# The last two tiles of a cross-attention stream in another order, and four weight splits on GpSimd

## The chip, the cores and the metric

The kernel runs on 1 core of one Trainium2 chip. The metric is the device time of one execution in microseconds.

## What is computed

A perceiver block: 256 query rows of 512 values (`x`), a context of 25088 rows of 512 values. Three residual steps, each on the layer-normalized `x`. The change touches the end of the first and the start of the second.

```python
x = x + xattn(layernorm(x), ctx, ctx, Wq, bq, Wk, bk, Wv, bv)   # sigmoid(qp kp^T / sqrt(128)) (ctx Wv^T + bv)
x = x + attn(layernorm(x), ...)    # 16 heads of 32, a shared rope part, causal softmax
x = x + ffn(layernorm(x), ...)     # 8 experts, the best one per row
```

The output must have float32 accuracy. The large matrix products therefore run on operands split into a high part, rounded to fp32r, and a low part (value minus high part), with three products: high by high, high by low, low by high.

## The kernel before

**The stream.** The context comes in 49 tiles (b = 0 to 48, `last` = 48) of 512 rows. Each is loaded twice, transposed (`rawt`) and as rows (`rawn`), each in two halves. For a tile the kernel

- splits the transposed tile into `th` (ScalarE, `copy`, line 401) and `tl` (VectorE, line 651), and the rows into `nh` (line 401) and `nl` (line 662);
- forms the keys on TensorE (`keys`, 12 matmuls of 512 columns) and splits them into `kph` (ScalarE, line 423) and `kpl` (VectorE, line 667);
- forms the scores against the queries (`scores`, 12 matmuls of 256 columns, banks 2 and 3: bank 2 holds context rows j = 0, 1, bank 3 holds j = 2, 3);
- takes the sigmoid into `zf` (ScalarE, line 432, one half for each bank), splits it into `zh` (line 401) and `zl` (VectorE, line 672), and adds `zf` to `zacc` (line 677), from which the sums of weights `zsum` come at the end;
- adds weights by context rows to the sums `y` (`value`): 4 row groups j, 2 halves r of the queries (bank 4 for r = 0, bank 5 for r = 1), 3 products i, so 24 matmuls of 512 columns.

All matmuls are issued by the helper `mm` and so have line 1009 in the profile. The second half of the context rows of tile 48 is split into `th` and `tl`, which are free by then.

**The order.** Each engine has one queue, filled in the order in which the program's block of that engine is written, with semaphore waits (`wait_ge`) between instructions; `Steps` only names the semaphore values. In the stream TensorE does scores(b), keys(b+1), values(b). At the end (lines 1160 on) the order is written out: `row_values(last - 1, 0)`, `scores(last)`, three products of row half 1 of tile 47, `last_values(0)` (12 products), four more of row half 1; then the sums of row half 0 go to `y_s` (ScalarE), are turned (`transposes`, line 1101), split into `yTh` and `yTl`, and multiplied by the value weights (`project_v(0)`), among the rest of row half 1's products. When the last product is done (`av1`), ScalarE copies row half 1 to `y_s` in two pieces, TensorE turns them (line 1229), then turns the normalized `h_s` of row half 0 (line 1101), then does `project_v(1)`.

**Behind the stream.** `norm_stats` and `norm_rows` (VectorE, with the square root `root` on ScalarE) give the normalized rows `h_s` from the projected sums; `latents` projects them; `query(t)` multiplies `hqh`, `hql` by the query weights, split into `wqh` (ScalarE) and `wql` (VectorE, line 682) while the stream ends; `query_copies` move the queries from PSUM into `qa`. The output weights `wo_s` are split into `woh` (ScalarE) and `wol` (VectorE, line 757) behind the stream and read by `project_o`. GpSimd only fills three tiles at the start (lines 394 to 396).

The DMA of `wo_s` waits on SyncE's queue for the last split of tile 48 (`n_split(last, 1)`); behind it stand the loads of the down weights `wds`. An activation of a function of another table than the last one loads the table (line 404, `table`, does it ahead of need).

Of the kernel before, what the change touches and what calls it, by code (L numbers as in the profile page):

```python
# [5 lines left out]
ALU = mybir.AluOpType  # L6
# [8 lines left out]
T = 256  # L15
# [39 lines left out]
def signals(nc, ctx, NB):  # L55
# [36 lines left out]
    s.zh, s.zl, s.za = (steps(n, tiles) for n in ("zh", "zl", "za"))  # L92
# [3 lines left out]
    s.zs, s.zs1, s.zr = (steps(n, ["z"]) for n in ("zs", "zs1", "zr"))  # L96
# [38 lines left out]
def program(nc, x, ctxn, ctxt, wkt, wqt, wvt, bqk, bv, kvd, kup, vup, wq, qrope, krope, wo, gate, wg, wu, wd,  # L135
# [3 lines left out]
    with ExitStack() as ctx:  # L139
# [252 lines left out]
        @block.gpsimd  # L392
        def _(e):
            e.memset(wz[:], 0.0).then_inc(*s.wz.mark("wz"))  # L394
            e.memset(zacc[:], 0.0).then_inc(*s.pz.mark("zacc"))
            e.memset(one_s[:], 1.0).then_inc(*s.pz.mark("one"))

        @block.scalar
        def _(e):
# [25 lines left out]
            def weights(b):  # L425
# [7 lines left out]
                e.wait_ge(*s.zf.of((b, 1)))  # L433
                copy(zh[b % 2][:], zf[:]).then_inc(*s.zh.mark(b))

            def query_weights(k):
# [5 lines left out]
                copy(flat(wqh[:, n]), flat(wq_s[:, n]), -0.125).then_inc(*s.wqh.mark(k))  # L442
# [23 lines left out]
            for b in range(NB - 1):  # L466
# [9 lines left out]
                split_n(b + 1, 0)  # L476
                split_n(b + 1, 1)
# [6 lines left out]
            weights(last)  # L484
# [27 lines left out]
            def query_copies(t, bk):  # L512
                e.wait_ge(*s.q.of(t))
                for i in (0, 2):
                    copy(qa[64 * (i % 2):64 * (i % 2) + 32, 2 * t + i // 2, :],
                         bank(bk)[32 * i:32 * i + 32, 0:T]).then_inc(*s.qaa.mark((t, i)))
# [4 lines left out]
            sum_turned(0, 0, slice(0, 4), 6)  # L521
            e.wait_ge(*s.dwo.of("w"))
            output_weights(0)
            root(0)
# [12 lines left out]
            root(1)  # L537
            e.wait_ge(*s.lnt.of((1, 3)))
# [9 lines left out]
            table(ACT.Exp)  # L548
# [95 lines left out]
        def _(e):  # L644
# [28 lines left out]

            def weight_sum(b):
# [3 lines left out]

            def query_weights(k):
                n = slice(2 * k, 2 * k + 2)  # L680
                e.wait_ge(*s.wqh.of(k))
                e.scalar_tensor_tensor(out=flat(wql[:, n]), in0=flat(wq_s[:, n]), scalar=-0.125, in1=flat(wqh[:, n]),
                                       op0=ALU.mult, op1=ALU.subtract).then_inc(*s.wql.mark(k))
# [35 lines left out]
            for b in range(NB - 1):  # L719
# [5 lines left out]
                if b + 2 < NB:  # L725
                    split_t(b + 2, 0)
                    split_t(b + 2, 1)
                split_n(b + 1, 0)
                split_n(b + 1, 1)
                if b >= NB - 3:  # L730
                    query_weights(b - (NB - 3))
# [4 lines left out]
            weights(last)  # L736
            weight_sum(last)
            e.wait_ge(*s.za.of(last))
            e.tensor_reduce(zsum[:], zacc[:].rearrange("p (j n) -> p n j", j=4), AX_X, ALU.add).then_inc(*s.zs.mark("z"))
# [13 lines left out]

            def output_weights(k):
                n = slice(2 * k, 2 * k + 2)
# [715 lines left out]
```

## Time and profile before

| | us |
|---|---|
| time, median of 3 runs | 574.36 (573.89 to 574.87) |
| profiled execution | 574.13 |
| span of the profiled execution | 572.3 |
| TensorE busy | 566.7 (99%) |
| VectorE busy | 462.9 (81%) |
| ScalarE busy | 403.1 (70%) |
| GpSimd busy | 1.7 |

The profile is that of one execution. Times in it are microseconds from the start of the span. In the page and the answers PE is TensorE's matmuls, PEld its weight loads, DVE is VectorE, ACT ScalarE, POOL GpSimd, SPq SyncE's DMA queue. The stream ends at about 487, the heads of the attention begin at about 505, and the experts run from 530 to the end.

### The profile page before, as it was taken

Reading aid. Unit: us, or ns where it says so; the run is one execution under the profiler, and the core shown is the slowest. Engines: PE = TensorE matmul, PEld = TensorE weight load, DVE = VectorE, ACT = ScalarE, POOL = GpSimd, SP = SyncE. Lnnn points to the kernel's source line nnn. Section 1 sums busy time; section 2 is a strip of 40 time slices with the busy share of each in tenths; the row PEclk is TensorE's granted clock in tenths of the full one; section 3 lists DMA queues with packets and bytes.
Section 4 is the critical chain, followed back from the end, with each engine's and each line's share of the span. In section 5 each row is a group of like instructions: output and inputs, shape, how many; then the busy total and the mean of one; then the engine's idle time right before and its main releaser. Section 6 shows DMA issues by size and latency. Waiting matters only on the chain.

```text
span 572.3 us, 8058 instructions
## 1 busy us (share of the span) xinstructions
PE 566.7 (99%) x2980; PEld 475.5 (83%) x2980; DVE 462.9 (81%) x520; ACT 403.1 (70%) x557; POOL 1.7 (0%) x7
## 2 busy tenths in 40 slices
PE   9999999999999999999999999999999999999998
PEld 5888888888888888888888888888888888777886
DVE  5987878787878888788879887878787879887685
ACT  6786767676767777778777777776767785598450
POOL 1000000000000000000000000000000000000000
PEclk9999999999999999999999999999999999999999
DMA  8568786777777777877787768676788663100201
GB/s 325 212 205 245 237 261 218 237 213 234 226 230 249 249 248 227 269 245 239 235 273 243 249 218 275 198 225 214 232 262 249 204 189 113 38 1 2 75 0 38
DMA packets 33239, 115.90 MB, mean 202 GB/s; under 512 B 4080, under 2 KB 4784, under 8 KB 32944
## 3 DMA queue, kind: packets, MB, share of 16 engines
q1 hardware_dynamic: 32768, 115.05, 63.2%
q8 instruction: 24, 0.39, 0.3%
q10 hardware_dynamic: 432, 0.33, 0.2%
q14 instruction: 15, 0.12, 0.1%
HBM read 114.84 MB, written 0.52 MB: 202 GB/s over the span
## 4 chain that ended last, share of the span: by engine, by line
PE 96%; ACT 2%; DVE 1%; issue 0%; POOL 0%; POOLq 0%
PE ps L1009 95%; ACT w L566 1%; PE ps L1101 0%; PE ps L1271 0%; DVE st L763 0%; DVE x_s L761 0%; DVE h_s L779 0%; DVE aTs L873 0%; DVE sm_s L850 0%; PE ps L1240 0%; ACT st L496 0%; ACT qk L401 0%; POOL wz L394 0%; DVE st L774 0%; DVE o_s L970 0%
## 5 line engine op out<-in xcount | busy, mean ns | idle before, releaser
L1009 PE MATMUL ps<-nh,zh 128*128 128x512 f32 x388 | 142.7, 390 | 0.0
L1009 PE MATMUL ps<-nl,zh 128*128 128x512 f32 x388 | 142.6, 389 | 0.0
L1009 PE MATMUL ps<-nh,zl 128*128 128x512 f32 x388 | 142.5, 389 | 0.0
L672 DVE TENSOR_TENSOR zl<-zf,zh 128x1024 fp32r<-128x1024 f32 x49 | 60.1, 1226 | 81.1 <-ACT zh L401 81.1
L662 DVE TENSOR_TENSOR nl<-rawn,nh 128x1024 fp32r<-128x1024 f32 x96 | 113.8, 1219 | 0.9 <-issue 0.6
L651 DVE TENSOR_TENSOR tl<-rawt,th 128x1024 fp32r<-128x1024 f32 x96 | 113.0, 1216 | 0.6 <-ACT th L401 0.4
L401 ACT ACTIVATE nh<-rawn 128x1024 fp32r<-128x1024 f32 x96 | 98.8, 1055 | 9.5 <-DMA rawn<-in_ctxn 8.8
L432 ACT ACTIVATE zf<-ps 128x512 f32<-128x512 f32 x98 | 58.5, 598 | 59.9 <-PE ps L1009 54.0
L401 ACT ACTIVATE th<-rawt 128x1024 fp32r<-128x1024 f32 x96 | 96.5, 1052 | 1.0 <-DMA rawt<-in_ctxt 0.8
L1009 PEld LDWEIGHTS ps<-nh,zl 128*128 128x128 f32 x388 | 72.8, 188 | 15.2
L1009 PEld LDWEIGHTS ps<-nl,zh 128*128 128x128 f32 x388 | 72.8, 188 | 15.1
L1009 PEld LDWEIGHTS ps<-nh,zh 128*128 128x128 f32 x388 | 72.6, 188 | 15.3 <-ACT zh L401 0.4
L423 ACT ACTIVATE kph<-ps,bqk_s 128x512 fp32r<-128x512 f32 x49 | 33.8, 691 | 48.6 <-PE ps L1009 48.5
L677 DVE TENSOR_TENSOR zacc<-zacc,zf 128x1024 f32<-128x1024 f32 x49 | 59.7, 1219 | 0.0
L1009 PE MATMUL ps<-qph,kpl 128*128 128x256 f32 x196 | 55.0, 283 | 0.0
L1009 PE MATMUL ps<-qpl,kph 128*128 128x256 f32 x196 | 54.9, 283 | 0.0
L1009 PE MATMUL ps<-qph,kph 128*128 128x256 f32 x196 | 54.8, 282 | 0.0
L1009 PE MATMUL ps<-th,wkh 128*128 128x512 f32 x196 | 53.9, 395 | 0.0
L401 ACT ACTIVATE zh<-zf 128x1024 fp32r<-128x1024 f32 x49 | 52.1, 1063 | 1.6
L1009 PE MATMUL ps<-tl,wkh 128*128 128x512 f32 x196 | 53.0, 391 | 0.0
L1009 PE MATMUL ps<-th,wkl 128*128 128x512 f32 x196 | 52.9, 390 | 0.0
L1009 PEld LDWEIGHTS ps<-th,wkl 128*128 128x128 f32 x196 | 36.8, 188 | 8.2
(188 smaller groups left out, 615.9 us busy)
## 6 DMA issues: line engine op xcount, KB each, us to landing
rawn<-in_ctxn SPq DMA_DIRECT2D x97, 512.0 KB, 6.3
rawt<-in_ctxt SPq DMA_DIRECT2D x96, 512.0 KB, 4.6
h_s<-in_wg SPq DMA_DIRECT2D x4, 512.0 KB, 6.9
h_s<-in_wu SPq DMA_DIRECT2D x4, 512.0 KB, 6.4
wds<-in_wd SPq DMA_DIRECT2D x4, 512.0 KB, 3.9
raw<-in_ctxt SPq DMA_DIRECT2D x2, 512.0 KB, 8.5
h_s<-in_wvt SPq DMA_DIRECT2D x2, 512.0 KB, 7.4
wq_s<-in_wq SPq DMA_DIRECT2D x1, 1024.0 KB, 9.3
```

Source lines behind the costliest of these rows:

```text
L401: return e.activation(dst, src, ACT.Copy, scale=scale)
L423: e.activation(kph[:], bank(b % 2), ACT.Identity, bias=bqk_s[:, 1:2]).then_inc(*s.kph.mark(b))
L432: e.activation(zf[:, gs], bank(2 + g), ACT.Sigmoid, scale=SC).then_inc(*s.zf.mark((b, g)))
L566: e.activation(w[:, n * c:n * c + n], sbank(p, u)[:, n * c:n * c + n], ACT.Exp, bias=sm_s[:, k, 4 + c:5 + c], scale=-1.0, accum_out=esum[: ...
L651: e.tensor_tensor(tl[:, n], raw_t(b)[:, n], th[:, n], ALU.subtract).then_inc(*s.tl.mark((b, k)))
L662: e.tensor_tensor(n_part(nl, tl, b, k), raw_n(b, k), n_part(nh, th, b, k), ALU.subtract).then_inc(*s.nl.mark((b, k)))
L672: e.tensor_tensor(zl[b % 2][:], zf[:], zh[b % 2][:], ALU.subtract).then_inc(*s.zl.mark(b))
L677: e.tensor_tensor(zacc[:], zacc[:], zf[:], ALU.add).then_inc(*s.za.mark(b))
L1009: return e.matmul(o, w, x, start=start, stop=stop)
```

## The change

1. *Scores of tile 48 earlier.* TensorE does `last_scores` behind four products of tile 47 (they were behind twelve), with the high key products of three row groups ahead of the first low one. ScalarE does `weights(last)` between the two halves of `split_n(last)`, and `zh` and `zl` of the last tile are made in two halves. VectorE takes `weight_sum(47)` ahead of `zl` of tile 47, and the last tile's subtracts in the new order.
2. *Row half 1 later.* Of tile 47's row half 1 only six products stand between row 0's last products and `transposes(y_s, 0)`, three follow these, three follow `project_v(0)`, and then come all twelve of tile 48. The turn of `h_s` row half 0 now stands ahead of the turn of row half 1's sums.
3. *GpSimd.* `wql` and `wol` are subtracted on GpSimd, `wol` behind the last query product (`q` of 3). The factor -0.125 moves from the query weights to the query copies.
4. *Smaller.* `zsum` comes from two adds instead of one reduce; `root(0)` stands ahead of `output_weights(0)`; the Exp table is loaded behind `root(1)`; on VectorE `sum_turned(1)` follows the copy of `hT`.

```diff
@@ -89,11 +89,12 @@
...
     s.s, s.zf = steps("s", halves), steps("zf", halves)
-    s.zh, s.zl, s.za = (steps(n, tiles) for n in ("zh", "zl", "za"))
+    s.zh, s.zl = (steps(n, [*range(last), (last, 0), (last, 1)]) for n in ("zh", "zl"))
+    s.za = steps("za", tiles)
     s.av, s.avh = (steps(n, range(NB - 2)) for n in ("av", "avh"))
...
     s.wqh, s.wql, s.woh, s.wol = (steps(n, range(2)) for n in ("wqh", "wql", "woh", "wol"))
-    s.zs, s.zs1, s.zr = (steps(n, ["z"]) for n in ("zs", "zs1", "zr"))
+    s.zs, s.zs1, s.zs2, s.zr = (steps(n, ["z"]) for n in ("zs", "zs1", "zs2", "zr"))
     s.xb = steps("xb", range(2))
@@ -394,6 +395,15 @@
...
             e.memset(one_s[:], 1.0).then_inc(*s.pz.mark("one"))
+            for k in range(2):
+                n = slice(2 * k, 2 * k + 2)
+                e.wait_ge(*s.wqh.of(k))
+                e.tensor_tensor(flat(wql[:, n]), flat(wq_s[:, n]), flat(wqh[:, n]), ALU.subtract).then_inc(*s.wql.mark(k))
+            e.wait_ge(*s.q.of(3))
+            for k in range(2):
+                n = slice(2 * k, 2 * k + 2)
+                e.wait_ge(*s.woh.of(k))
+                e.tensor_tensor(flat(wol[:, n]), flat(wo_s[:, n]), flat(woh[:, n]), ALU.subtract).then_inc(*s.wol.mark(k))
 
@@ -430,8 +440,12 @@
...
                     e.activation(zf[:, gs], bank(2 + g), ACT.Sigmoid, scale=SC).then_inc(*s.zf.mark((b, g)))
-                e.wait_ge(*s.zf.of((b, 1)))
-                copy(zh[b % 2][:], zf[:]).then_inc(*s.zh.mark(b))
+                    if b == last:
+                        e.wait_ge(*s.zf.of((b, g)))
+                        copy(zh[b % 2][:, gs], zf[:, gs]).then_inc(*s.zh.mark((b, g)))
+                if b < last:
+                    e.wait_ge(*s.zf.of((b, 1)))
+                    copy(zh[b % 2][:], zf[:]).then_inc(*s.zh.mark(b))
 
@@ -439,7 +453,7 @@
...
                 n = slice(2 * k, 2 * k + 2)
-                copy(flat(wqh[:, n]), flat(wq_s[:, n]), -0.125).then_inc(*s.wqh.mark(k))
+                copy(flat(wqh[:, n]), flat(wq_s[:, n])).then_inc(*s.wqh.mark(k))
 
@@ -474,6 +488,8 @@
...
                 split_n(b + 1, 0)
+                if b == NB - 2:
+                    weights(last)
                 split_n(b + 1, 1)
@@ -481,7 +497,6 @@
...
                     copy(ups[i][1], wst).then_inc(*s.uph.mark(i))
-            weights(last)
 
@@ -513,15 +528,15 @@
...
                     copy(qa[64 * (i % 2):64 * (i % 2) + 32, 2 * t + i // 2, :],
-                         bank(bk)[32 * i:32 * i + 32, 0:T]).then_inc(*s.qaa.mark((t, i)))
+                         bank(bk)[32 * i:32 * i + 32, 0:T], -0.125).then_inc(*s.qaa.mark((t, i)))
 
...
             sum_turned(0, 0, slice(0, 4), 6)
+            root(0)
             e.wait_ge(*s.dwo.of("w"))
             output_weights(0)
-            root(0)
             e.wait_ge(*s.av1.of("y"))
@@ -535,6 +550,7 @@
...
             root(1)
+            table(ACT.Exp)
             e.wait_ge(*s.lnt.of((1, 3)))
@@ -545,7 +561,6 @@
...
             value_copy(0, 6)
-            table(ACT.Exp)
             e.wait_ge(*s.k.of(1))
@@ -671,16 +686,16 @@
...
 
+            def last_weights(g):
+                gs = slice(512 * g, 512 * g + 512)
+                e.wait_ge(*s.zh.of((last, g)))
+                e.tensor_tensor(zl[last % 2][:, gs], zf[:, gs], zh[last % 2][:, gs],
+                                ALU.subtract).then_inc(*s.zl.mark((last, g)))
+
             def weight_sum(b):
...
                 e.tensor_tensor(zacc[:], zacc[:], zf[:], ALU.add).then_inc(*s.za.mark(b))
-
-            def query_weights(k):
-                n = slice(2 * k, 2 * k + 2)
-                e.wait_ge(*s.wqh.of(k))
-                e.scalar_tensor_tensor(out=flat(wql[:, n]), in0=flat(wq_s[:, n]), scalar=-0.125, in1=flat(wqh[:, n]),
-                                       op0=ALU.mult, op1=ALU.subtract).then_inc(*s.wql.mark(k))
 
@@ -716,27 +731,32 @@
...
             split_t(1, 1)
-            for b in range(NB - 1):
+            for b in range(NB - 2):
                 weights(b)
...
                 key_part(b + 1)
-                if b + 2 < NB:
-                    split_t(b + 2, 0)
-                    split_t(b + 2, 1)
+                split_t(b + 2, 0)
+                split_t(b + 2, 1)
                 split_n(b + 1, 0)
                 split_n(b + 1, 1)
-                if b >= NB - 3:
-                    query_weights(b - (NB - 3))
                 i = up_turn(b)
...
                     e.tensor_tensor(ups[i][2], wst, ups[i][1], ALU.subtract).then_inc(*s.upl.mark(i))
-            weights(last)
+            weight_sum(last - 1)
+            weights(last - 1)
+            key_part(last)
+            split_n(last, 0)
+            last_weights(0)
+            last_weights(1)
+            split_n(last, 1)
             weight_sum(last)
             e.wait_ge(*s.za.of(last))
-            e.tensor_reduce(zsum[:], zacc[:].rearrange("p (j n) -> p n j", j=4), AX_X, ALU.add).then_inc(*s.zs.mark("z"))
+            e.tensor_tensor(zacc[:, 0:512], zacc[:, 0:512], zacc[:, 512:1024], ALU.add).then_inc(*s.zs2.mark("z"))
+            e.wait_ge(*s.zs2.of("z"))
+            e.tensor_tensor(zsum[:], zacc[:, 0:T], zacc[:, T:512], ALU.add).then_inc(*s.zs.mark("z"))
 
@@ -751,11 +771,6 @@
...
 
-            def output_weights(k):
-                n = slice(2 * k, 2 * k + 2)
-                e.wait_ge(*s.woh.of(k))
-                e.tensor_tensor(flat(wol[:, n]), flat(wo_s[:, n]), flat(woh[:, n]), ALU.subtract).then_inc(*s.wol.mark(k))
-
             def norm_stats(m, bk):
@@ -807,8 +822,8 @@
...
                 for i in (1, 3):
-                    e.tensor_copy(qa[64 * (i % 2):64 * (i % 2) + 32, 2 * t + i // 2, :],
-                                  bank(bk)[32 * i:32 * i + 32, 0:T]).then_inc(*s.qav.mark((t, i)))
+                    e.tensor_scalar(qa[64 * (i % 2):64 * (i % 2) + 32, 2 * t + i // 2, :],
+                                    bank(bk)[32 * i:32 * i + 32, 0:T], -0.125, None, ALU.mult).then_inc(*s.qav.mark((t, i)))
 
@@ -818,15 +833,13 @@
...
                                        op0=ALU.mult, op1=ALU.add).then_inc(*s.xb.mark(r))
-            output_weights(0)
             e.wait_ge(*s.xp.of(0))
...
             norm_rows(0)
-            sum_turned(1)
             e.wait_ge(*s.lnt.of(0))
             e.tensor_scalar(hT[:, :, half(0)], chunks(0), 2.0, None, ALU.mult).then_inc(*s.lne_v.mark(0))
-            output_weights(1)
+            sum_turned(1)
             query_low(0)
@@ -1043,7 +1056,7 @@
...
                 return mm(bank(4 + r), z[b % 2][:, j * T + r * P:j * T + r * P + P], n,
-                          (b, i, j) == (0, 0, 0), (b, r, i, j) in ((last, 0, 1, 3), (last, 1, 2, 3)))
+                          (b, i, j) == (0, 0, 0), (b, i, j) == (last, 2, 3))
 
@@ -1074,27 +1087,20 @@
...
 
-            def row_values(b, r, js, waits):
-                for i in (0, 2, 1):
-                    if waits:
-                        value_waits(b, 0, i)
-                    for j in (0, 1):
-                        value(b, j, r, i)
-                for j in js:
-                    for i in range(3):
-                        if waits and j == 2 and i != 1:
-                            value_waits(b, 1, i)
-                        value(b, j, r, i)
-
-            def last_values(r):
-                for i in (0, 2, 1):
-                    for j in range(4):
-                        if j == 0:
-                            value_waits(last, 0, i)
-                        if j == 2 and i != 1:
-                            value_waits(last, 1, i)
-                        m = value(last, j, r, i)
-                return m
+            def last_scores():
+                e.wait_ge(*s.kph.of(last))
+                e.wait_ge(*s.zf.of((last - 1, 1)))
+                for i, j in ((0, 0), (1, 0), (0, 1), (1, 1), (0, 2), (1, 2), (2, 0), (2, 1), (0, 3), (1, 3), (2, 2), (2, 3)):
+                    if (i, j) == (2, 0):
+                        e.wait_ge(*s.kpl.of(last))
+                    m = score(last, i, j)
+                    if (i, j) in ((2, 1), (2, 3)):
+                        m.then_inc(*s.s.mark((last, j // 2)))
+
+            def last_waits(k, i):
+                if i != 1:
+                    e.wait_ge(*(s.nl if i else s.nh).of((last, k)))
+                e.wait_ge(*(s.zl if i == 1 else s.zh).of((last, k)))
 
@@ -1157,13 +1163,34 @@
...
                     values(b)
-            row_values(last - 1, 0, (2, 3), True)
-            scores(last)
-            row_values(last - 1, 1, (2,), False)
-            last_values(0).then_inc(*s.av0.mark("y"))
-            for i in range(3):
-                value(last - 1, 3, 1, i)
-            value(last, 0, 1, 0)
+            for i in (0, 2):
+                value_waits(last - 1, 0, i)
+                for j in (0, 1):
+                    value(last - 1, j, 0, i)
+            last_scores()
+            value_waits(last - 1, 0, 1)
+            for j in (0, 1):
+                value(last - 1, j, 0, 1)
+            for j in (2, 3):
+                for i in range(3):
+                    if j == 2 and i != 1:
+                        value_waits(last - 1, 1, i)
+                    value(last - 1, j, 0, i)
+            rows = [(j, i) for j in range(4) for i in range(3)]
+            for i in (0, 2, 1):
+                last_waits(0, i)
+                for j in (0, 1):
+                    value(last, j, 0, i)
+            for i in (0, 1, 2):
+                last_waits(1, i)
+                for j in (2, 3):
+                    m = value(last, j, 0, i)
+                if i == 1:
+                    for j, i_ in rows[:2]:
+                        value(last - 1, j, 1, i_)
+            m.then_inc(*s.av0.mark("y"))
+            for j, i in rows[2:6]:
+                value(last - 1, j, 1, i)
 
@@ -1206,8 +1233,8 @@
...
             transposes(y_s, 0, 6).then_inc(*s.yt.mark(0))
-            value(last, 0, 1, 2)
-            value(last, 0, 1, 1)
+            for j, i in rows[6:9]:
+                value(last - 1, j, 1, i)
             e.wait_ge(*s.zs.of("z"))
@@ -1215,23 +1242,21 @@
...
             e.wait_ge(*s.zf.of((last, 1)))
-            value(last, 1, 1, 0)
             project_v(0, 2)
-            value(last, 1, 1, 1)
-            value(last, 1, 1, 2)
-            for j in (2, 3):
-                for i in range(3):
-                    m = value(last, j, 1, i)
+            for j, i in rows[9:]:
+                value(last - 1, j, 1, i)
+            for j, i in rows:
+                m = value(last, j, 1, i)
             m.then_inc(*s.av1.mark("y"))
+            e.wait_ge(*s.lnh.of(0))
+            e.wait_ge(*s.zr.of("z"))
+            transposes(h_s, 0, 0).then_inc(*s.lnt.mark(0))
             for k in range(4):
...
                     m.then_inc(*s.yt.mark((1, k // 2)))
-            e.wait_ge(*s.lnh.of(0))
-            e.wait_ge(*s.zr.of("z"))
-            transposes(h_s, 0, 0).then_inc(*s.lnt.mark(0))
             project_v(1, 3)
...
             latents(0, 1, 2, 4, 6)
```

## Rows read from the trace of the kernel before

**Rows 1.** The page: busy us, share, instructions; granted clock in 40 slices.

```profile
PE 566.7 (99%) x2980; PEld 475.5 (83%) x2980; DVE 462.9 (81%) x520; ACT 403.1 (70%) x557; POOL 1.7 (0%) x7
...
PEclk9999999999999999999999999999999999999999
```

**Rows 2.** The chain that ended last: start us, us, what.

```profile
485.54 0.70 DVE x_s L761
...
488.20 0.56 DVE h_s L779
```

**Rows 3.** TensorE's waits from 440 to the end: us in total, times, longest.

```profile
PE ps L1229 <- ACT h_s L401: 0.5, 1, 0.5
PE ps L1101 <- DVE h_s L779: 0.4, 2, 0.2
```

**Rows 4.** Timeline of TensorE, 471 to 487: start us, us, instruction.

```profile
471.11 0.62 PE L1009 MATMUL ps<-nh,zh 128*128 128x512 f32 x2
...
472.02 0.62 PE L1009 MATMUL ps<-nh,zl 128*128 128x512 f32 x2
...
473.83 0.28 PE L1009 MATMUL ps<-qph,kph 128*128 128x256 f32 x1
...
475.14 0.28 PE L1009 MATMUL ps<-qph,kpl 128*128 128x256 f32 x1
...
486.93 0.39 PE L1009 MATMUL ps<-tl,zh 128*128 128x512 f32 x1
```

**Rows 5.** Timeline of ScalarE and VectorE, 467 to 475.

```profile
467.01 1.22 DVE L662 TENSOR_TENSOR nl<-rawn,nh 128x1024 fp32r<-128x1024 f32 x1
...
468.56 0.60 ACT L432 ACTIVATE zf<-ps 128x512 f32<-128x512 f32 x1
...
470.16 1.04 ACT L401 ACTIVATE wqh<-wq_s 128x1024 fp32r<-128x1024 f32 x1
470.29 1.23 DVE L672 TENSOR_TENSOR zl<-zf,zh 128x1024 fp32r<-128x1024 f32 x1 [0.92 <-ACT zh L401]
...
471.31 0.69 ACT L423 ACTIVATE kph<-ps,bqk_s 128x512 fp32r<-128x512 f32 x1
...
472.57 0.75 DVE L667 SCALAR_TENSOR_TENSOR kpl<-ps,bqk_s,kph 128x512 fp32r<-128x512 f32 x1
...
473.28 1.06 ACT L401 ACTIVATE th<-rawn 128x1024 fp32r<-128x1024 f32 x1 [0.33 <-DMA rawn<-in_ctxn]
```

**Rows 6.** Groups by form, 466 to 508: busy us, mean ns of one, idle before.

```profile
L784 DVE TENSOR_TENSOR hq<-hT,hq 128x512 fp32r<-128x512 f32 x2 | 1.4, 678 | 0.0
...
L401 ACT ACTIVATE hq<-hT 128x512 fp32r<-128x512 f32 x2 | 1.3, 626 | 0.1
```

**Rows 7.** DMA issues, 455 to 500 (KB, us to landing), and GpSimd's timeline.

```profile
wo_s<-in_wo SPq DMA_DIRECT2D x1, 1024.0 KB, 4.7
...
1.19 0.95 POOL L395 MEMSET zacc<- 128x1024 f32 x1
```

**Rows 8.** Timeline around the end of the stream, 487 to 493.

```profile
487.42 0.64 ACT L401 ACTIVATE h_s<-ps 128x256 f32<-128x256 f32 x2
...
487.83 0.71 PE L1229 MATMUL ps<-id_s,h_s 128*128 128x128 f32 x4 [0.52 <-ACT h_s L401]
...
488.31 0.66 ACT L401 ACTIVATE yTh<-ps 128x256 fp32r<-128x256 f32 x2 [0.25 <-PE ps L1229]
...
488.80 0.66 PE L1101 MATMUL ps<-id_s,h_s 128*128 128x128 f32 x4 [0.25 <-DVE h_s L779]
...
489.21 1.17 PE L1009 MATMUL ps<-wvh,yTh 128*128 128x512 f32 x4
...
492.26 0.69 DVE L761 TENSOR_TENSOR x_s<-ps,x_s 128x512 f32<-128x512 f32 x1 [0.34 <-PE ps L1009]
```

**Rows 9.** Timeline ahead of the attention's heads, 500 to 506.

```profile
500.66 1.28 ACT L404 ACT_TABLE_LOAD   x1
...
505.25 1.16 PE L1009 MATMUL ps<-qk 64*128 64x128 f32 x16 [0.20 <-issue]
```

## The prediction

> **What bounds the kernel now.** I read the page's busy times first: TensorE is busy 99% of the span, and its granted clock is 1.00 throughout, the 2.4 GHz level [rows 1]. So only two things can shorten the run: fewer matmuls, or the removal of time in which TensorE stands still. Next the chain of waits: through the stream it is TensorE alone, and it leaves TensorE first at 485.5, through the layer norm of query row 0 on VectorE and ScalarE, until `h_s` is written at 488.76 [rows 2]. The list of TensorE's waits names the place: 0.5 us at line 1229, for ScalarE's copy of the second row's sums, and 0.4 us in two waits at line 1101 for VectorE's normalized rows [rows 3], of which the one here is 0.25 [rows 8].
>
> The timeline of TensorE gives the price of a product: 471.11 to 472.02 is four 128x512 matmuls, 0.227 us from start to start; twelve score matmuls start between 473.83 and 475.14, 0.119 us apart [rows 4]. From 471.11 (first product of tile 47) to 486.93 (last product of the stream) there is no stall: the sum of its instructions fills it.
>
> **The tail part by part.** The number of matmuls is the same before and after; they are only ordered anew. What can change is (1) stalls that the new order brings before the last product, and (2) the idle time behind it. I follow the three engines through the new order with the durations of the old.
>
> *Scores earlier.* TensorE now does four products of tile 47 (0.91 us, to 472.02) and then the twelve scores. These need `kph`, which ScalarE writes at 471.31 + 0.69 = 472.00 [rows 5]; with 0.05 us of hand-over they start at about 472.1: a stall of 0.08. The first six need only `kph` and run until 472.81. The seventh needs `kpl`. VectorE no longer has two `wql` subtracts of 1.22 us; its queue is `zacc` (waits for `zf`, whose second half ScalarE ends at 469.16, then 1.22, to 470.4), `zl` of tile 47 (470.3 to 471.5, as before at 470.29), `kpl` at 472.04, 0.75 long, so to 472.79 [rows 5]: it was at 472.57 before. Stall 0.03. So scores end by 473.57; the first bank is complete at 473.25 and the second at 473.73.
>
> ScalarE: first half of tile 48's `nh` to 472.95 as before; `zf` half 0 from 473.29 (0.60), `zh` half 0 (a 128x512 rounding copy takes 0.63, [rows 6]) to 474.52, `zf` half 1 to 475.1, `zh` half 1 to 475.73, then the second half of the context rows, which ran at 473.28 before and takes 1.06 [rows 5], to 476.70. Then a table load of 1.28 [rows 9] with its dummy until 478.2. VectorE: `nl` half 0 from 473.0 to 474.2, `zl` halves (0.68 each, [rows 6]) to 475.2 and 476.4, `tl` (the low second half, 1.23) from 476.75 to 477.97, `zacc` to 479.1, and the two adds that replace the reduce.
>
> TensorE against these: eight products of tile 47 from 473.57 to 475.38; then row 0 of tile 48 in pairs of 0.45. Pair 1 at 475.38 (needs `zh` half 0, 474.52), pair 2 at 475.84 (`nl`, 474.2), pair 3 at 476.29 (`zl` half 0, 475.2), pair 4 at 476.75 (the copy that ends at 476.70: stall 0.05), pair 5 at 477.25 (`zl` half 1, 476.4), two of tile 47, pair 6 at 478.16 (`tl`, 477.97). The sums of row 0 are complete at 478.8, ScalarE copies them by 479.4, and TensorE, which has four products of row 1 until 479.5, turns them with no stall. Then three products, the `zsum` matmuls and `project_v(0)` follow; `zsum` is done at about 480.2, needed at 480.6. So row 0's projection begins at about 481.1, and the last product starts at 486.93 plus the three stalls, 0.16: at 487.09. Bounds of that: 0 (each of the three is within 0.1 us of vanishing) and 0.5 (every hand-over on these tight edges 0.1 longer).
>
> *Behind the last product.* Fifteen products now stand between `project_v(0)` and the end of the stream, eight before. Row 0's projection is therefore readable at 487.09 + 0.23 - 15 x 0.227 + 0.16 = 484.08. Its norm took from 485.54 to 488.76, 3.22 us [rows 2], and nothing blocks it: `wol`'s subtract has left VectorE, and ScalarE's `root(0)` now stands ahead of `output_weights(0)`, which would otherwise wait for `wo_s`. That load is issued behind `n_split(last, 1)`, so 2.3 us later than at 475.7, and lands 4.7 after issue [rows 7], at 482.7; its reader comes at 486.0. Behind it on SyncE's queue stand only the down weights, read after 536. So `h_s` row 0 is ready at 487.3 and its four transposes start at once, in the hole in which TensorE waited.
>
> ScalarE's copies of row 1's sums start at 487.52 instead of 487.42: the product ends 0.16 later, but in the old order `root(0)` held ScalarE until 487.4. Row 1's transposes start at 487.93 instead of 487.83, and `yTh` (0.66 for two, from 488.31) moves to 488.41 [rows 8]. `project_v(1)` waits for the first of them, 488.79, instead of for the `h_s` transposes: it starts at 488.86 instead of 489.21 [rows 8]. **The gain is 0.35 us**, and what is late next is ScalarE's copy and turn of row 1. Its bounds: 0 (the two edges each 0.17 worse) and 0.75 (the two waits of 0.52 and 0.25 in [rows 8] gone entirely, which the copy forbids).
>
> *Does it arrive?* Everything up to the attention hangs on `project_v(1)`: its norm on VectorE started at 492.26 and now can at 491.9. VectorE's `query_low(0)` waits for ScalarE's `hqh(0)`, at about 491.15, and ends at 491.88: it just lets it through. From there the norm, rope and query copies of VectorE lead to the head scores at 505.25 [rows 9], and all move by the same 0.35. The table load of Exp, 1.28 at 500.66 [rows 9], goes into a hole in which ScalarE waits for the turned rows; but VectorE, not ScalarE, sets 505.25, so it is worth nothing. The scale -0.125 moves into copies out of PSUM whose instruction is the same on ScalarE and a `tensor_scalar` instead of a copy on VectorE: zero, bounds -0.1 and +0.1 per stage. After 505 nothing is changed but `wol`, which TensorE needs at 525.
>
> *GpSimd.* Four subtracts of 128x1024 come to it; the trace has none. The nearest rows are its fill of 128x1024 at 0.95 us [rows 7] and VectorE's subtract of this shape at 1.22 [rows 5]. Two operands against none: I take 1.9 us (two passes of 0.95), from 0.95 to 2.85 (three). `wql` is ready by 475 and read at 500.9, `wol` by about 512 and read at 525. By time alone the cost is nothing; the cover would be gone from 12 us apiece.
>
> A sentence apart: the Trainium skill, "GPSIMD Engine Reference", section 3.1, gives 4.5 us for 2048 elements of a two-input operation, which would be an estimate of 2.25 for 1024; no row here shows it.
>
> **Sum.** Profiled execution 574.13 (span 572.34, 1.8 around it) - 0.35 = 573.78; the median of the three runs lies 0.23 above the profiled one, so 574.36 - 0.35 = **574.0**. This change is smaller than what a measurement of this kernel tells from no change, about 0.2% or 1.15 us.
>
> **Rivals.** *Clean re-ordering* (as summed): 574.0, 50%.
>
> *GpSimd and VectorE exclude each other, VectorE keeps its turn*, 22%. The first `wql` subtract becomes ready while VectorE's `nl` runs (to 468.2, [rows 5]). If the two cannot run together it goes 468.2 to 470.1, `zacc` to 471.4, `zl` to 472.5, `kpl` to 473.2: TensorE stalls 0.4 at the seventh score instead of 0.03. The second goes 472.5 to 474.4, `nl` half 0 ends at 475.6 and is needed at 476.2. Net 0.0: 574.4. At 2.85 apiece the stall is 1.3 and `nl` adds 0.4: net +1.35, 575.7.
>
> *The same, and GpSimd takes the lock between two VectorE operations*, 13%: this is the case on the slow side. The second subtract is ready at 471.25 (its high part is written from 470.16, 1.04 long, [rows 5]). If it starts at 471.3, when `zacc` ends, `zl` goes 473.2 to 474.4 and `kpl` to 475.15; the seventh score stalls 2.35, all of it on TensorE. Net +2.0: 576.4. It decides from the point where `kpl` comes later than 473.3. For it: VectorE has an operation with two SBUF operands on either side of both subtracts. Against: VectorE's next operation already overlaps the one before by 0.1 us, so it may keep the port. The trace of before has no overlap of the two engines and cannot tell.
>
> Beside this stands a rule of the Trainium skill, "SBUF — State Buffer", section "Who interferes with whom": a VectorE instruction with two SBUF inputs and a GpSimd instruction that reads SBUF block each other for a whole instruction, whichever is issued first. By that rule one of the two rivals above holds; if GpSimd's subtract takes 2.25 us, as in the estimate, they come out at about 574.8 and 577.1.
>
> *The edit does not do what it says*: the hole closes, but `query_low(0)` or a later wait gives it all back, 574.3, 10%. *More than the sum*: no stalls ahead of the end, the full 0.75 and a shorter VectorE chain, 573.4, 5%.
>
> **Chances.** Faster by over 0.2% (below 573.2) has no mechanism but an odd case: 0.06. Slower (above 575.5): the lock taken by GpSimd, and part of the milder lock: 0.16. Same: 0.78. The range leaves out the worst lock: 573.3 to 575.7.
>
> **What the profile would show.** If right: TensorE's scores of tile 48 at 472.1 with a gap under 0.1 at the seventh; the `h_s` transposes at 487.3 and no wait at line 1101; `project_v(1)` 0.35 earlier, and that 0.35 unchanged at the head scores. If a lock: VectorE's `zacc` at 470 instead of 469.2, its subtracts beside GpSimd's longer than 1.22 or started at GpSimd's ends, and a wait of TensorE for VectorE's `kpl`. The prediction falls if the four subtracts last over 3 us beside VectorE, or if head scores do not move with `project_v(1)`.

## The result

| | before | changed |
|---|---|---|
| time, median of 7 runs, us | 574.36 (573.84 to 574.87) | 577.15 (576.34 to 578.43) |
| ratio | | 1.0054, 95% interval 1.0044 to 1.0063 |
| profiled execution, us | 574.13 | 577.21 |
| span of it, us | 572.3 | 575.4 |

The change makes the kernel slower by 0.5%, which is 2.5 to 3.6 us. The forecast was 574.0 with a range to 575.7. The measured time lies where the prediction had put its worst rival: GpSimd and VectorE exclude each other, and GpSimd gets its turn between two VectorE operations (576.4 by the rows, about 577.1 with the estimate from the Trainium skill, "GPSIMD Engine Reference", section 3.1).

The page of the changed kernel: TensorE is busy as long as before (566.7) in a longer span, and GpSimd has 10 us of work.

```profile
span 575.4 us, 8067 instructions
...
PE 566.7 (98%) x2980; PEld 475.4 (83%) x2980; DVE 461.7 (80%) x518; ACT 405.9 (71%) x558; POOL 11.7 (2%) x11
```

TensorE's waits between 440 and 512 (us in total, times, longest). Against [rows 3] the waits for the copy of row 1's sums and for `h_s` are gone or small, and one for `kpl` is new:

```profile
PE ps L1022 <- DVE kpl L682: 2.6, 1, 2.6
PE ps L1022 <- ACT yTh L411: 0.2, 1, 0.2
PE ps L1022 <- issue: 0.2, 1, 0.2
```

The chain that ended last, from 460 on, no longer stays on TensorE through the end of the stream. It leaves it for 6.4 us of VectorE's queue; for 1.83 of them, inside `zl`'s duration, the view names no cause (`issue`):

```profile
468.70 2.38 DVE zacc L698
471.09 1.41 DVE zl L687
472.50 1.83 issue
474.33 0.75 DVE kpl L682
475.08 0.04 issue
475.13 6.97 PE ps L1022 x32
```

The timelines of GpSimd, VectorE and ScalarE in the same stretch (start, us, instruction) say why. In [rows 5] `zl` takes 1.23 us, and `zacc` behind it, in the same trace, 1.22:

```profile
471.43 1.22 DVE L677 TENSOR_TENSOR zacc<-zacc,zf 128x1024 f32<-128x1024 f32 x1
```

In the changed kernel:

```profile
467.18 2.82 POOL L401 TENSOR_TENSOR wql<-wq_s,wqh 128x1024 fp32r<-128x1024 f32 x1 [465.00 <-ACT wqh L411]
470.80 2.54 POOL L401 TENSOR_TENSOR wql<-wq_s,wqh 128x1024 fp32r<-128x1024 f32 x1 [0.79 <-ACT wqh L411]
510.46 4.67 POOL L406 TENSOR_TENSOR wol<-wo_s,woh 128x1024 fp32r<-128x1024 f32 x2 [37.13 <-PE ps L1022]
...
465.39 2.35 DVE L677 TENSOR_TENSOR nl<-rawn,nh 128x1024 fp32r<-128x1024 f32 x2
468.70 2.38 DVE L698 TENSOR_TENSOR zacc<-zacc,zf 128x1024 f32<-128x1024 f32 x1 [0.96 <-ACT zf L442]
471.01 3.40 DVE L687 TENSOR_TENSOR zl<-zf,zh 128x1024 fp32r<-128x1024 f32 x1
474.33 0.74 DVE L682 SCALAR_TENSOR_TENSOR kpl<-ps,bqk_s,kph 128x512 fp32r<-128x512 f32 x1
...
470.82 0.69 ACT L433 ACTIVATE kph<-ps,bqk_s 128x512 fp32r<-128x512 f32 x1
```

GpSimd's first subtract ends at 470.00 and VectorE's `zacc`, begun at 468.70, ends 1.08 later, at 471.08. GpSimd's second ends at 473.34 and `zl`, begun at 471.01, ends 1.07 later, at 474.41. Both record their wait as busy time. `kph` was there at 471.51, `kpl` only at 475.07. The two `wol` subtracts, with no such neighbour, take 2.33 each.

**The measure for the experiments.** The two profiled spans differ by 3.1 us, but not all of that is the change's. The first product of tile 47 comes at 470.62 in the changed kernel and at 471.11 before [rows 4], because the start was 0.5 faster (the warm-up matmuls took 7.18 instead of 7.67), and behind the last VectorE operation the span goes on for 3.1 us instead of 2.1. I therefore compare a stage inside the trace, from the first product of tile 47 to the first head-score matmul: 34.14 us before (471.11 to 505.25), 36.64 in the changed kernel (470.62 to 507.26). The change costs 2.50 there, and nothing between the head scores and the last operation (64.98 and 64.99 us from one to the other). 2.50 is at the lower end of the interval of the timed ratio (2.5 to 3.6). The medians differ by 2.8; two of the changed kernel's seven runs, the longest (578.18 and 578.43), had a granted clock of 0.997, and the other five, at 1.00, have a median of 576.64, 2.3 above the kernel before.

### The profile page after: what moved, and what is told of

Its sections match the earlier page's. It is cut to its first block, busy times and chain, and to the rows that moved or that the text cites. A ratio compares the mean times of both kernels' runs of the same rounds, so it can differ in the third digit from the quotient of the medians.

```text
span 575.4 us, 8067 instructions
## 1 busy us (share of the span) xinstructions
PE 566.7 (98%) x2980; PEld 475.4 (83%) x2980; DVE 461.7 (80%) x518; ACT 405.9 (71%) x558; POOL 11.7 (2%) x11
## 4 chain that ended last, share of the span: by engine, by line
PE 95%; ACT 2%; DVE 2%; issue 1%; POOL 0%; POOLq 0%
PE ps L1022 94%; ACT w L581 1%; PE ps L1296 0%; DVE zacc L698 0%; PE ps L1107 0%; DVE zl L687 0%; DVE kpl L682 0%; DVE st L778 0%; DVE x_s L776 0%; DVE sm_s L863 0%; DVE aTs L886 0%; PE ps L1265 0%; ACT zf L442 0%; ACT qk L411 0%; POOL wz L395 0%
## 5 line engine op out<-in xcount | busy, mean ns | idle before, releaser
L411 ACT ACTIVATE nh<-rawn 128x1024 fp32r<-128x1024 f32 x96 | 100.6, 1059 | 14.0 <-DMA rawn<-in_ctxn 12.5
L698 DVE TENSOR_TENSOR zacc<-zacc,zf 128x1024 f32<-128x1024 f32 x49 | 60.9, 1243 | 1.0 <-ACT zf L442 1.0
L411 ACT ACTIVATE zh<-zf 128x1024 fp32r<-128x1024 f32 (+1 forms) x50 | 52.3, 1046 | 1.6
```

The lines of the kernel that those rows point to most:

```text
L411: return e.activation(dst, src, ACT.Copy, scale=scale)
L698: e.tensor_tensor(zacc[:], zacc[:], zf[:], ALU.add).then_inc(*s.za.mark(b))
```

## The experiments

Theory 1: the two engines exclude each other for whole instructions when both read SBUF. Theory 2: it is the new order of VectorE (`zacc` ahead of `zl` ahead of `kpl`) that makes `kpl` late. "Stage" is the stretch measured above: 34.14 us before, 36.64 in the changed kernel. Times are medians with the ratio to the kernel before and its 95% interval.

### wql back on VectorE (wql_dve)

```diff
 # GpSimd: the two wql subtracts out
 # VectorE
+            query_weights(0)
             weight_sum(last - 1)
...
             e.tensor_tensor(zsum[:], zacc[:, 0:T], zacc[:, T:512], ALU.add)
+            query_weights(1)
```

> The changed kernel with the two wql subtracts back on VectorE: the first where it was (behind nl of tile 47), the second behind zsum, where VectorE is idle; wol stays on GpSimd. Measure beside the time: the stage from the first product of tile 47 to the first head-score matmul, 34.14 us in before (471.11 to 505.25) and 36.64 in the changed kernel (470.62 to 507.26). Theory 1, GpSimd and VectorE exclude each other when both read SBUF: kpl is ready in time again, the stall of 2.6 us at the seventh score of tile 48 goes, the rest of the change is worth 0.35: stage 33.8, time 574.0. Theory 2, the new order of VectorE (zacc ahead of zl ahead of kpl) is itself late: the stall stays, stage 36 or more, time 576.5 or more.

Measured: 574.34 us, ratio 1.0001 (0.9992 to 1.0010), stage 33.93. VectorE's timeline, same columns:

```profile
467.90 1.22 DVE L699 TENSOR_TENSOR wql<-wq_s,wqh 128x1024 fp32r<-128x1024 f32 x1
469.04 1.22 DVE L694 TENSOR_TENSOR zacc<-zacc,zf 128x1024 f32<-128x1024 f32 x1
470.17 1.22 DVE L683 TENSOR_TENSOR zl<-zf,zh 128x1024 fp32r<-128x1024 f32 x1
471.79 0.75 DVE L678 SCALAR_TENSOR_TENSOR kpl<-ps,bqk_s,kph 128x512 fp32r<-128x512 f32 x1 [0.40 <-ACT kph L429]
```

With one more operation in the same queue, `zacc` and `zl` are back at 1.22 and `kpl` waits for ScalarE again. The order is not at fault: the two subtracts on GpSimd cost 2.71 of the stage (36.64 against 33.93). The rest of the change is worth 0.21 us in the stage, where 0.35 was forecast; the timed runs are too coarse to show it, since their interval goes from 0.5 us faster to 0.6 slower than the kernel before.

### Only wql on GpSimd, in the old order (old_pool)

```diff
 # the kernel before; GpSimd
+            for k in range(2):
+                n = slice(2 * k, 2 * k + 2)
+                e.wait_ge(*s.wqh.of(k))
+                e.tensor_tensor(flat(wql[:, n]), flat(wq_s[:, n]), flat(wqh[:, n]), ALU.subtract)
 # VectorE: query_weights out; -0.125 in the query copies
```

> The kernel before with only one part of the change: the two wql subtracts on GpSimd (the factor -0.125 moved to the query copies), everything else in the old order. Theory 1 (exclusion): the first subtract runs from 468.2 to about 470.6, zl of tile 47 from there to 471.7, the second subtract waits since 471.3 and takes the turn until 474.1, zacc until 475.2, kpl until 475.9, needed at 474.06: a stall of about 1.9 us, time 576.3. Theory 2 (the new order is at fault): no stall, VectorE has 2.4 us less work, time 574.4.

Measured: 575.47, ratio 1.0025 (1.0016 to 1.0035), stage 35.99: 1.85 more than before, from this one part alone, as theory 1 had it (1.9). In time it is 0.9 to 2.0 us more, and the forecast 576.3 was too high.

```profile
467.59 2.56 POOL L400 TENSOR_TENSOR wql<-wq_s,wqh 128x1024 fp32r<-128x1024 f32 x1 [465.40 <-ACT wqh L405]
470.71 2.80 POOL L400 TENSOR_TENSOR wql<-wq_s,wqh 128x1024 fp32r<-128x1024 f32 x1 [0.56 <-ACT wqh L405]
...
469.72 1.51 DVE L676 TENSOR_TENSOR zl<-zf,zh 128x1024 fp32r<-128x1024 f32 x1 [1.84 <-ACT zh L405]
471.15 3.43 DVE L681 TENSOR_TENSOR zacc<-zacc,zf 128x1024 f32<-128x1024 f32 x1
474.51 0.74 DVE L671 SCALAR_TENSOR_TENSOR kpl<-ps,bqk_s,kph 128x512 fp32r<-128x512 f32 x1
```

The operation that is held longest is now `zacc`, because it is the one issued while GpSimd's second subtract waits or runs; `zl` is held by the first, 0.3. TensorE's new wait is for `kpl`, 1.6 us. Theory 2 had forecast no stall.

### Only the second subtract on GpSimd (second_pool)

```diff
 # GpSimd
-            for k in range(2):
+            for k in (1,):
 # VectorE
+            query_weights(0)
             weight_sum(last - 1)
# TensorE's wait for both halves of wql is written anew
```

> The changed kernel with the first wql subtract on VectorE (where it was) and only the second on GpSimd. Theory 1: GpSimd's subtract becomes ready at 471.2 while zl of tile 47 runs, goes from 471.5 to 473.9; kpl (one operand in PSUM, one in SBUF) is not held by it and is ready at 472.8; nl half 0 is held until 473.9 and ends at 475.1, needed at 475.8: no stall, time 574.0, stage 33.8. If an operation with one SBUF operand is held as well, kpl comes at 474.6 and TensorE stalls 1.8: 575.8.

Measured: 573.78, ratio 0.9997 (0.9988 to 1.0007), stage 33.91.

```profile
471.26 2.62 POOL L402 TENSOR_TENSOR wql<-wq_s,wqh 128x1024 fp32r<-128x1024 f32 x1 [469.07 <-ACT wqh L412]
...
470.39 1.22 DVE L688 TENSOR_TENSOR zl<-zf,zh 128x1024 fp32r<-128x1024 f32 x1
472.01 0.75 DVE L683 SCALAR_TENSOR_TENSOR kpl<-ps,bqk_s,kph 128x512 fp32r<-128x512 f32 x1 [0.40 <-ACT kph L434]
473.01 1.95 DVE L678 TENSOR_TENSOR nl<-rawn,nh 128x1024 fp32r<-128x1024 f32 x1 [0.25 <-ACT nh L412]
```

`kpl`, with one operand in PSUM, keeps its 0.75 in the middle of GpSimd's subtract; `nl`, with two in SBUF, is held to 1.08 behind GpSimd's end at 473.88. As nobody waits for `nl` yet, it costs nothing.

### Only the first on GpSimd (first_pool)

```diff
 # GpSimd
-            for k in range(2):
+            for k in (0,):
 # VectorE, behind zsum
+            query_weights(1)
```

> The changed kernel with only the first wql subtract on GpSimd, the second on VectorE behind zsum. By exclusion: zacc of tile 47 is held until GpSimd ends (ends 1.1 after it, as in the changed kernel at 471.08), zl follows at once to 472.2, kpl 472.2 to 472.9, needed at 472.4: TensorE stalls about 0.5 at the seventh score, stage 34.5, time 574.7. This is the milder of the two lock cases of the prediction; with both subtracts on GpSimd it was 36.64, with only the second 33.91, so the two stalls would not add up but the second needs the first.

Measured: 574.64, ratio 1.0014 (1.0005 to 1.0024), stage 34.49, TensorE's wait for `kpl` 0.4. So the first subtract alone costs 0.58 against second_pool (0.56 against wql_dve), the second alone nothing, both together 2.7. The first pushes `zacc`'s end (471.08 in the changed kernel) past the moment at which the second is issued (470.80), and so `zl` stands behind it; without the first, `zl` is issued ahead of it.

### The subtracts in pieces (pieces)

```diff
             for k in range(2):
-                n = slice(2 * k, 2 * k + 2)
...
+                for i in range(4):
+                    n = slice(1024 * k + 256 * i, 1024 * k + 256 * i + 256)
+                    m = e.tensor_tensor(flat(wql[:])[:, n], flat(wq_s[:])[:, n], flat(wqh[:])[:, n], ALU.subtract)
+                m.then_inc(*s.wql.mark(k))
```

> The changed kernel with each of GpSimd's two wql subtracts cut into four of 256 columns (2.33 / 4 = 0.58 us each, perhaps 0.65 with the fixed part), nothing else changed. If the two engines exclude each other for a whole instruction and the one that was issued first goes first: each VectorE operation waits for at most one piece, zacc ends at about 470.5 and zl at about 472.2 (on the clock of the changed kernel's trace, where they ended at 471.1 and 474.4), kpl at 472.9, needed at 472.4: stage 34.4 instead of 36.64, time about 574.6. If GpSimd keeps the port between its instructions: zacc, zl and kpl come as late as in the changed kernel, stage 36.6.

Measured: 574.63, ratio 1.0016 (1.0006 to 1.0026), stage 34.41.

```profile
467.42 9.68 POOL L402 TENSOR_TENSOR wql<-wq_s,wqh 128x256 fp32r<-128x256 f32 x8 [465.23 <-ACT wqh L413]
...
468.73 1.42 DVE L700 TENSOR_TENSOR zacc<-zacc,zf 128x1024 f32<-128x1024 f32 x1 [0.97 <-ACT zf L444]
470.07 1.76 DVE L689 TENSOR_TENSOR zl<-zf,zh 128x1024 fp32r<-128x1024 f32 x1
```

Each VectorE operation now waits for one piece at most: 0.2 and 0.5 us on top of 1.22, instead of 1.2 and 2.2. Four fifths of the loss is gone with the same work on the same engine. GpSimd does not keep VectorE out between its instructions: the two now take turns, and GpSimd's own work is spread over 9.68 us, where two whole subtracts took 2.82 and 2.54. It is still 0.48 behind the subtracts on VectorE (33.93).

### Six fills instead of the subtracts (fills)

```diff
 # wql_dve; GpSimd
+            e.wait_ge(*s.upl.of(9))
+            for i in range(6):
+                e.wait_ge(*s.wqh.of(i // 3))
+                if i:
+                    e.wait_ge(*s.fl.of(i - 1))
+                e.memset(wst, float(i)).then_inc(*s.fl.mark(i))
```

> The kernel wql_dve (all wql subtracts on VectorE, no stall, stage 33.93 us), with six fills of 128x1024 on GpSimd (0.95 each, into a tile that is free then) at the moments of its two subtracts: three from about 467.3, three from about 470.9, beside VectorE's wql subtract, zacc, zl and nl, all with two operands in SBUF. If only operations that read SBUF exclude each other: VectorE's durations stay at 1.22, stage 33.9. If any GpSimd operation holds VectorE: its durations grow to 2 and more, kpl comes late, stage 35 or more.

One run, 574.88 us: stage 33.94; `zacc` and `zl` at 1.22 beside fills of 3.11 us for three (the trace names the filled tile `h_s`).

```profile
466.95 3.11 POOL L404 MEMSET h_s<- 128x1024 f32 x3 [464.76 <-ACT wqh L414]
...
468.75 1.22 DVE L702 TENSOR_TENSOR zacc<-zacc,zf 128x1024 f32<-128x1024 f32 x1
```

GpSimd's fills, which only write, hold nobody. What the subtracts add is work on operands that they read from SBUF; together with `kpl`, which has one operand in PSUM and is not held (second_pool), that points to the reading of SBUF.

### wql behind the stream (wql_late)

```diff
 # GpSimd, the changed kernel
+            e.wait_ge(*s.zs.of("z"))
             for k in range(2):
```

> The changed kernel with GpSimd's wql subtracts held back until zsum is written (about 480), so that nothing of GpSimd lies beside the splits of the stream. Theory 1: the stall at the seventh score goes, but the subtracts (2.35 each) now meet VectorE's two additions to x_s with two operands in SBUF (481.5 to 482.9 in my sum): the second of them waits until about 485.4, the norm of row 0 and with it h_s come 2.0 later, time about 575.7. If exclusion is only a matter of the splits of the stream, or if GpSimd's place and not its overlap were the cause: 574.0.

Measured: stage 35.85, 1.94 over second_pool, with the wait in the place that was expected (`h_s`, 2.02). The stall in the stream is gone; two additions to `x_s` take 4.50 together, where they take 1.42 in wql_norm. The median is 577.20, not 575.7, ratio 1.0059 (1.0042 to 1.0075), from four runs only. That is more than the 1.7 us of the stage over the kernel before. The profiled run, 576.04, is 1.8 over; why the other three are longer is not explained.

```profile
481.69 4.50 DVE L835 SCALAR_TENSOR_TENSOR x_s<-bv_s,zcol,x_s 128x512 f32<-128x512 f32 x2
...
489.55 0.66 PE L1108 MATMUL ps<-id_s,h_s 128*128 128x128 f32 x4 [2.02 <-DVE h_s L795]
```

### wql beside the layer norm (wql_norm)

```diff
+            e.wait_ge(*s.xb.of(1))
             for k in range(2):
```

> The changed kernel with GpSimd's wql subtracts held back until VectorE has written x_s (about 483.3): they run until about 488, beside VectorE's layer norm, whose operations have one operand in SBUF (bn_stats, the normalizing tensor_scalar of 0.55) or one in PSUM and one in SBUF (the residual addition). If only two SBUF operands count: no operation is stretched, stage 33.9, time 574.0, as good as on VectorE. If the normalizing tensor_scalar is held too: h_s at 488.6 instead of 487.4, TensorE waits about 0.9 more, stage 34.8, time 575.0.

Measured: 575.05, ratio 1.0020 (1.0008 to 1.0032), stage 35.11. Neither case as written. The addition of the projected sums (0.69, one operand in PSUM) and `bn_stats` (0.69, one operand) are untouched; an operation of a single element for each row, whose operands all lie in SBUF, takes 1.57 us instead of 0.22, as in wql_late:

```profile
483.08 4.74 POOL L402 TENSOR_TENSOR wql<-wq_s,wqh 128x1024 fp32r<-128x1024 f32 x2 [480.89 <-DVE x_s L835]
...
484.80 0.69 DVE L779 BATCH_NORM_STATS2 st<-x_s 128x6 f32<-128x512 f32 x1
...
486.27 1.57 DVE L790 SCALAR_TENSOR_TENSOR st<-st 128x1 f32<-128x1 f32 x1
...
488.07 0.55 DVE L795 TENSOR_SCALAR h_s<-x_s,st 128x512 f32<-128x512 f32 x1
```

I had looked at operations by size and missed it. `h_s` came at 488.6, the very time I had given for another reason. Whether the normalizing `tensor_scalar` is held, this run does not say: it began at 488.07, when GpSimd had ended, at 487.82.

### wol without its wait (wol_early)

```diff
 # wql_dve; GpSimd
-            e.wait_ge(*s.q.of(3))
```

> The kernel wql_dve without GpSimd's wait for the last query product, so that the two wol subtracts run as soon as ScalarE has the high parts. By exclusion: the first goes from 486.9 to 489.3, beside VectorE operations with at most one operand in SBUF (h_s, hT, yTl), which keep their durations; the second goes from 489.9 to 492.3 and holds the low part of hq (two operands in SBUF, ready at 491.1), so that the addition to x_s of row 1 starts at about 493.0 instead of 491.8: stage 35.1, time 575.5. If the wait is not needed: stage 33.9, time 574.3.

Measured: 575.28, ratio 1.0018 (1.0008 to 1.0027), stage 34.92: 0.99 over wql_dve. The addition to `x_s` of row 1 starts at 492.61, in wql_dve at 491.82, because the low part of `hq` in front of it takes 1.85 instead of 0.69.

```profile
489.75 2.39 POOL L401 TENSOR_TENSOR wol<-wo_s,woh 128x1024 fp32r<-128x1024 f32 x1 [0.57 <-ACT woh L406]
...
490.83 1.85 DVE L801 TENSOR_TENSOR hq<-hT,hq 128x512 fp32r<-128x512 f32 x1 [1.60 <-ACT hq L406]
```

### wol beside the rope copies (wol_mid)

```diff
 # second_pool; GpSimd
-            e.wait_ge(*s.q.of(3))
+            e.wait_ge(*s.k.of(1))
```

> The kernel second_pool (stage 33.91) with GpSimd's wol subtracts released by the key product of row 1 (about 499.7) instead of the last query product, so that they lie beside VectorE's four copies of the rope part, 32x2048 from SBUF to SBUF, 1.22 each, which are twice as fast by element as its other operations (2048 in 1.22 against 1024). If such a fast copy excludes GpSimd: the copies at 501.9 and 504.9 are held or stretched by one to two us, or GpSimd's subtracts are, and the stage grows by about 1.0 to 34.9. If only two SBUF operands count: stage 33.9 and all durations as before.

One run, 578.83 us: stage 37.19, 3.28 over second_pool, where 1.0 was expected.

```profile
500.10 5.55 POOL L407 TENSOR_TENSOR wol<-wo_s,woh 128x1024 fp32r<-128x1024 f32 x2 [25.84 <-PE ps L1029]
...
501.80 1.60 DVE L819 TENSOR_TENSOR rt<-rt 32x256 f32<-32x256 f32 x1
503.44 3.30 DVE L827 COPY qk<-rt 32x2048 f32<-32x2048 f32 x1
```

The fast copy with a single SBUF operand is held (3.30 for 1.22, to 1.09 behind GpSimd's end at 505.65). My price was too low because I had left out the small addition of 0.41 ahead of it: it is held by GpSimd's first subtract (1.60), and the copy then comes behind the second, 1.2 and 2.1 us in a row. The same cascade as in the changed kernel.

Not tried: handing row 1's sums over in two column halves, to shorten what is late next. ScalarE would read a PSUM bank while TensorE still writes it, and the program orders nothing between them; without another bank it would not be free of races.

## Why the prediction was wrong, point by point

**The views and the bound: right.** TensorE bounds the kernel, its work is the same (566.7 us in both), and only stalls count. Both stalls in [rows 3] that the change aimed at went: TensorE turns `h_s` 0.28 behind the last product's start, where it was 1.87 behind it [rows 4, 8].

**The clean sum: right in mechanism, too large.** 0.35 was forecast; wql_dve and second_pool give 0.21 and 0.23. From the first product of tile 47 to the last it takes 16.08 and 16.06 us instead of 15.82 [rows 4]: 0.25 of stalls instead of the 0.16 of the sum. The rest of the way, to `project_v(1)`, is as summed: it starts 1.77 behind the last product's start in both (488.73 and 488.91), 2.28 before [rows 4, 8]. From there to the head scores it is 16.07 and 16.08 against 16.04. What is late next is ScalarE's `yTh`, as said, 0.2.

**"By time alone the cost is nothing": true and beside the point.** The subtract of 128x1024 takes 2.33 alone, inside the bounds of 0.95 to 2.85, above the 1.9 I took; the Trainium skill's "GPSIMD Engine Reference", section 3.1, gives 4.5 for 2048. An estimate of 2.25 for this one follows from it, close to what the trace has.

**The step that failed: the two `wql` subtracts on GpSimd, put at nothing.** The sum priced them by their own duration, beside VectorE and without effect on it. They cost 2.71 us of the stage: 36.64 with both on GpSimd, 33.93 with both on VectorE and the rest of the change in place. The exclusion stood among the rivals, but the choice between them was wrong. I gave 50% to an overlap without any exclusion, 22% to an exclusion in which VectorE keeps its turn and 13% to the one that came, which the range left out. The trace of before could not speak for the first: GpSimd and VectorE meet in it only once, in fills at the start (0.06 and 0.07 us on VectorE beside 0.52 on GpSimd), which the prediction had overlooked when it wrote that they never overlap. The rule of the Trainium skill, "SBUF — State Buffer", section "Who interferes with whom", spoke against it, and I left the exclusion a third of the chance. The traces here agree with that rule (an exclusive lock for a whole instruction, two SBUF inputs against a reading GpSimd): 2.38 and 3.40 for 1.22; writes alone hold nobody (fills); a PSUM operand frees the instruction (`kpl`, 0.75). The copy of 32x2048 in wol_mid, with one SBUF operand, was held too (3.30).

**And within it, the turn.** My reason for "VectorE keeps its turn" was that VectorE's next operation overlaps the one before by 0.1. In the trace GpSimd's second subtract was issued at 470.80 and `zl` at 471.01, and the earlier one went first. The prediction had both moments in hand (GpSimd ready at 471.25, `zacc` ending at 471.3) and treated the order as a matter of chance. It can go the other way too: in pieces `zacc`, issued at 468.73, went ahead of the piece issued at 469.03. No trace here shows a held operation that was passed by one issued later. But an engine issues its next operation only when its last one is done, but for 0.1 us, so that a mere taking of turns would give the same order in each of these cases; the two are not told apart.

**The size.** For that rival I had a stall of 2.35 and net +2.0. The changed kernel shows a stall of 2.75 (the seventh score at 475.13, due at 472.38) and a stage longer by 2.50. The main part of the difference is the duration: 2.33 of work for each subtract, where I had 1.9. A part of that comes back, because a held operation ends 1.07 behind GpSimd's end and not 1.22.

**What held besides.** The later load of `wo_s` and `root(0)` ahead of it, the moved table load and the -0.125 in the query copies (1.79 for four on VectorE, before and after) show no wait of their own. No run takes them out one by one; from `project_v(1)` to the head scores, where the table load and the query copies lie, the way is 16.07 against 16.04.

## What to carry to other kernels

An idle engine is not free room: before work is moved to GpSimd, list VectorE's operations in that window that read two SBUF operands, or copy SBUF to SBUF fast, however small they are, and ask which of them the bottleneck waits for; place the work beside operations that read PSUM. If it must lie in a busy stretch, cut it in short pieces, since a neighbour waits for one whole instruction: quartering took the stage from 36.64 to 34.41. Here the best place was none of these: with the subtracts left on VectorE the stage is 33.93, and 33.91 with only the second one on GpSimd. And where the trace has no overlap of two engines, the case that they exclude each other deserves at least the chance of the case that they do not; who went first followed, in every case here, from the issue times.

## What the runs showed of the hardware that I had not expected

- A VectorE operation that is held shows the wait inside its own duration and not as idle time in front: `zl` 3.40 for 1.22. The list of waits does not name GpSimd at all; only the duration against its usual one gives it away.
- The size of the held operation does not matter: 128x1 took 1.57 instead of 0.22 (wql_norm), 32x256 took 1.60 instead of 0.41 (wol_mid).
- A held operation of 128x1024 ends 1.07 to 1.08 behind GpSimd's end (zacc, zl, nl), about 0.15 sooner than its usual duration.
- It works in both directions: VectorE's running `nl` also lengthened GpSimd's first subtract, to 2.82 from 2.33.
- Two holds in a row are more than the sum of each alone: 0.58 and 0.0 alone, 2.7 together.
